# Adaptive layer norm, local attention and a mixture of experts: the set-up of the first batch and a program of its own for batch 0

## The reference

```python
mod = (_silu(L0_c) @ L0_wmod).reshape(L0_c.shape[0], 6, 1, -1)
sa, ca, ga, sb, cb, gb = (mod[:, 0], ..., mod[:, 5])
ga = (2 * (ga >= 0) - 1) * jnp.maximum(jnp.abs(ga), 0.25)
...
h = _layernorm(x, axis=-1) * (1 + ca) + sa
x_tran = jnp.matmul(h, W) + b
weights = jnp.einsum('bsd,btd->bst', x_tran, h)
lw = 1.0 / (location + EPS) * (location != 0)      # location = |i - j|
weights = jnp.exp(jnp.tanh(weights * lw))
weights = weights * off_diag
weights = weights / (jnp.sum(weights, axis=-1, keepdims=True) + EPS)
x = x + ga * jnp.matmul(weights, h)
h = _layernorm(x, axis=-1) * (1 + cb) + sb
x = x + gb * ffn(h)                                # top 2 of 8 experts, and a shared one
```

## Time and profile before

| | us |
|---|---|
| median of 3 runs | 718.41 |
| the three runs | 720.79, 718.41, 714.60 |
| the profiled execution | 714.96 |
| its span | 713.2 |
| PE busy | 633.7 (89%) |
| DVE busy | 472.6 (66%) |
| ACT busy | 400.2 (56%) |
| POOL busy | 371.6 (52%) |

### The profile page before, as it was taken

The page is one execution under the profiler, slowest core; times in us unless marked ns, Lnnn a source line. Parts: engine busy times, 40 slices in busy tenths (PEclk is TensorE's granted clock), DMA queues, the critical chain, the costliest instruction groups (busy, mean ns, idle before and its releaser), DMA issues.

```text
span 713.2 us, 13455 instructions
## 1 busy us (share of the span) xinstructions
PE 633.7 (89%) x4311; PEld 576.9 (81%) x4311; DVE 472.6 (66%) x1455; ACT 400.2 (56%) x639; POOL 371.6 (52%) x353
## 2 busy tenths in 40 slices
PE   2599898798888888887977999999999999999995
PEld 2398787688787777777966889998999899999995
DVE  6678997795959688686957357454454445444498
ACT  4568678474765757463531365556556555655441
POOL 4415254667566567577657126565655555556200
PEclk9889999898998999998987999999999999999998
DMA  8030000000010101010113726565666566530692
GB/s 302 0 150 1 1 2 23 15 31 31 24 37 20 35 12 39 23 39 31 35 45 113 259 84 205 175 201 166 202 188 199 185 184 203 168 105 31 233 372 118
DMA packets 29612, 76.44 MB, mean 107 GB/s; under 512 B 7110, under 2 KB 11358, under 8 KB 29440
## 3 DMA queue, kind: packets, MB, share of 16 engines
q1 hardware_dynamic: 20208, 58.49, 25.1%
q0 software_dynamic: 8640, 16.93, 6.7%
q10 hardware_dynamic: 720, 0.47, 0.2%
HBM read 53.53 MB, written 23.24 MB: 108 GB/s over the span
## 4 chain that ended last, share of the span: by engine, by line
PE 41%; DVE 33%; ACT 11%; issue 6%; another core or an unknown queue 6%; POOL 1%; DMA 1%; POOLq 0%; ACTq 0%; DVEq 0%; SPq 0%
PE value L1550 13%; PE score L1404 6%; PE score L1402 6%; PE score L1403 6%; PE misc L1550 6%; DVE work L957 5%; DVE stats L862 3%; ACT work L687 3%; ACT work L685 3%; PE value L1597 2%; PE value L1430 2%; DVE rows_all L980 2%; ACT w_ring L663 1%; DVE rows_all L945 1%
## 5 line engine op out<-in xcount | busy, mean ns | idle before, releaser
L632 POOL DMA_INDIRECT rows_z<-tile_y,tags x142 | 146.1, 1029 | 124.4 <-issue 42.9
L957 DVE TENSOR_TENSOR work<-score,lw 128x1024 f32<-128x1024 f32 x64 | 78.1, 1220 | 43.7 <-remote 30.1
L1430 PEld LDWEIGHTS value<-w_ring,work 128*128 128x128 f32 x768 | 98.3, 202 | 7.0 <-DVE work L963 3.5
L1402 PE MATMUL score<-h_hi,h_lo 128*128 128x512 f32 (+1 forms) x252 | 95.6, 380 | 8.2 <-issue 4.7
L1430 PE MATMUL value<-w_ring,work 128*128 128x129 f32 x768 | 99.3, 286 | 1.6 <-DVE work L963 1.6
L563 POOL DMA_INDIRECT rows_x<-work,slot x64 | 67.0, 1047 | 47.0 <-DVE work L957 15.5
L685 ACT ACTIVATE work<-work 128x1024 f32<-128x1024 f32 x64 | 67.3, 1052 | 43.0 <-DVE work L957 41.1
L1404 PE MATMUL score<-h_hi,h_lo 128*128 128x512 f32 (+1 forms) x252 | 90.1, 357 | 0.0
L1403 PE MATMUL score<-h_hi,h_lo 128*128 128x512 f32 (+1 forms) x252 | 89.8, 356 | 0.0
L769 ACT ACTIVATE work<-score,w_ring 128x512 f32<-128x512 f32 (+1 forms) x96 | 53.4, 617 | 61.5 <-PE score L1404 54.4
L769 ACT ACTIVATE work<-score,w_shared 128x512 f32<-128x512 f32 x64 | 40.3, 687 | 59.5 <-PE score L1404 29.7
(11 more groups left out here) (238 smaller groups left out, 1303.6 us busy)
## 6 DMA issues: line engine op xcount, KB each, us to landing
w_ring<-packs SPq DMA_DIRECT2D x24, 578.0 KB
rows_all<-packs SPq DMA_DIRECT2D x23, 578.0 KB
lw<-rows_x SPq DMA_DIRECT2D x24, 260.0 KB
res<-x SPq DMA_DIRECT2D x8, 512.0 KB, 5.6
h_t<-rows_z SPq DMA_DIRECT2D x4, 1024.0 KB, 8.0
mod<-mod_rows SPq DMA_DIRECT2D x1, 2560.0 KB, 10.2
rows_z<-tile_y,tags POOLq DMA_INDIRECT x142
rows_all<-rows_z SPq DMA_DIRECT2D x2, 1024.0 KB, 12.7
```

What stands on the lines that cost most here:

```text
L632: nc.gpsimd.indirect_dma_start(rows_z[:, :], bass.IndirectOffsetOnAxis(ap=tags[pos][:, k, 0:1].bitcast(I32), axis=0), tile_y[par][:, k, :] ...
L957: nc.vector.tensor_tensor(prob[:, t % 4, :].rearrange("p (h n) -> p h n", h=2), score[:, 2 * (t % 2):2 * (t % 2) + 2, :], lw[:, at:at + S] ...
L1402: nc.tensor.matmul(out, a_lo, b_hi, start=True, stop=False)
L1430: ins = nc.tensor.matmul(value[:, s // 3, c0:c0 + D + 1], prob[:, t % 4, s * P:(s + 1) * P], normal[b % 3][:, t, :], start=(t == 0 and s % ...
```

## The change

In the set-up, the 1024 columns of the reciprocals are cut into pieces of 128, 256, 256 and 384 columns (before 256, 384 and 384), and the last of them is moved behind the instructions that write `mod_col`. With the small one for the silu these are five reciprocals. The attention weight's high part (`watt_hi`) is written by ACT before the keys of batch 0, not after them. The moments of batch 1 and the shift formed from them go from ahead of the first `weigh` to behind the first and the second.

Batch 0 has a function of its own, `first_batch`, on ACT, DVE and PE, and the conditions on b == 0 in `batch` are gone. POOL's and SP's programs are the same.

```diff
@@ -699,19 +699,33 @@
                 act.wait_ge(gap_ready, b + 1)
                 nc.scalar.activation(gap_e[:, :], gap[:, :], ACT.Exp).then_inc(gap_exp, 1)
 
+            def first_batch(par):
+                weights(0, 0)
+                modulation()
+                weights(0, 1)
+                normalise(1)
+                weights(0, 2)
+                weights(0, 3)
+                transposed(1, 1 - par, 0)
+                weights(0, 4)
+                transposed(1, 1 - par, 1)
+                weights(0, 5)
+                queries(1, 1 - par, 0)
+                weights(0, 6)
+                queries(1, 1 - par, 1)
+                weights(0, 7)
+                normalise(2)
+
             def batch(b, par):
-                ahead_2 = [(0, 2), (2, 4), (4, 6), (6, 8)] if 0 < b < B - 2 else []
-                if exists(b + 1) and b > 0:
+                if b == 0:
...
-                if b == 0:
-                    normalise(b + 2)
 
             normalise(0, 0, G // 2)
             normalise(0, G // 2, G)
+            act.wait_ge(small_loaded, 48)
+            nc.scalar.activation(watt_hi[:, :], watt_sb[:, :], ACT.Copy).then_inc(watt_hi_ready, 1)
             act.wait_ge(col_ready, 1)
             for half in range(2):
                 transposed(0, 0, half, score[:, half, :])
-            act.wait_ge(small_loaded, 48)
-            nc.scalar.activation(watt_hi[:, :], watt_sb[:, :], ACT.Copy).then_inc(watt_hi_ready, 1)
             for half in range(2):
                 queries(0, 0, half, score[:, 2 + half, :])
             batches(act, batch)
@@ -889,7 +901,7 @@
             dve.wait_ge(distance_ready, 1)
             lw_chain(nc.vector.scalar_tensor_tensor(out=lw_from[:, :], in0=lw_from[:, :], scalar=-1.0, in1=lw_from[:, :], op0=ALU.mult, op1=ALU.max))
             lw_chain(nc.vector.tensor_scalar(lw_from[:, :], lw_from[:, :], EPS_ATT, None, ALU.add))
-            location_weights(0, 2 * P)
+            location_weights(0, P)
             moments_1(0)
 
             step = Chain(dve, silu_step, 0)
@@ -897,13 +909,14 @@
             step(nc.vector.tensor_scalar(silu[:, :], silu[:, :], 1.0, None, ALU.add))
             step(nc.vector.reciprocal(silu[:, :], silu[:, :]))
             nc.vector.tensor_tensor(silu[:, :], silu[:, :], c_sb[:, :], ALU.mult).then_inc(silu_ready, 1)
-            location_weights(2 * P, 5 * P)
+            location_weights(P, 3 * P)
             shift_1(0, 1)
-            location_weights(5 * P, S)
+            location_weights(3 * P, 5 * P)
 
             dve.wait_ge(col_ps_ready, 1)
             nc.vector.tensor_copy(mod_col[:, 0:2, :].rearrange("p m b -> p (m b)"), misc[:, 0:2 * B])
             nc.vector.tensor_scalar(mod_col[:, 2:4, :].rearrange("p m b -> p (m b)"), misc[:, 2 * B:4 * B], 1.0, None, ALU.add).then_inc(col_ready, 1)
+            location_weights(5 * P, S)
 
             def mirror(i):
 
@@ -932,10 +945,8 @@
             mirror(0)
             for half in range(2):
                 split_q(0, 0, half, score[:, 2 + half, :])
-            moments_1(1)
             dve.wait_ge(const_ready, 1)
             nc.vector.memset(den[:, :], 0.0)
-            shift_1(1, 2)
 
             def normalise_2(b, to=xhat2):
                 dve.wait_ge(ln2_rstd, b + 1)
@@ -1063,12 +1074,42 @@
                 dve.wait_ge(w_hi_ready, m + 1)
                 nc.vector.tensor_tensor(w1_lo[par], w[:, 0:F], w1_hi[par].bitcast(F32), ALU.subtract).then_inc(w_split, 1)
 
+            def first_batch(par):
+
+                weigh(0, 0)
+                moments_1(1)
+                weigh(0, 1)
+                shift_1(1, 2)
+                weigh(0, 2)
+                weigh(0, 3)
+                moments_1(2)
+                clear_diagonal(0, 0)
+                weigh(0, 4)
+                split_h(1, 1 - par, 0)
+                clear_diagonal(0, 1)
+                clear_diagonal(0, 2)
+                weigh(0, 5)
+                split_h(1, 1 - par, 1)
+                shift_1(2, 3)
+                clear_diagonal(0, 3)
+                weigh(0, 6)
+                split_q(1, 1 - par, 0)
+                moments_1(3)
+                clear_diagonal(0, 4)
+                weigh(0, 7)
+                split_q(1, 1 - par, 1)
+                moments_1(4)
+                clear_diagonal(0, 5)
+                clear_diagonal(0, 6)
+                clear_diagonal(0, 7)
+
+
             def batch(b, par):
+                if b == 0:
+                    return first_batch(par)
                 weigh(b, 0)
                 if exists(b - 2):
                     count_chosen(b - 2, route_chain[b - 2])
-                if b == 0:
-                    moments_1(2)
                 if b == 1:
                     moments_1(AHEAD)
                     shift_1(3, AHEAD)
@@ -1090,8 +1131,6 @@
                     moments_2(b - 1)
                 if exists(b + 1):
                     split_q(b + 1, 1 - par, 0)
-                if b == 0:
-                    moments_1(3)
                 if b == 1:
...
+                scores(0, par, 5)
+                values(0, par, 2)
+                queries(1, 1 - par, 0)
+                scores(0, par, 6)
+                values(0, par, 3)
+                queries(1, 1 - par, 1)
+                values(0, par, 4)
+                scores(0, par, 7)
+                values(0, par, 5)
+
             def batch(b, par):
-
-
+                if b == 0:
+                    return first_batch(par)
                 scores(b, par, 0)
                 if exists(b - 1):
                     values(b - 1, 1 - par, G - 2)
-                if b > 0 and exists(b + 1):
+                if exists(b + 1):
                     transpose_h(b + 1, 0)
                 scores(b, par, 1)
                 if exists(b - 1):
@@ -1465,13 +1521,8 @@
                         pe.wait_ge(ht_ready, 2 * b + 3)
                     ranks(b - 2)
                 scores(b, par, 2)
-                if b == 0:
-                    pe.wait_ge(mirrored, 2)
-                    transpose_h(1, 0)
                 if exists(b + 1):
                     transpose_h(b + 1, 1)
-                if b == 0:
-                    pe.wait_ge(mod_evac, 1)
                 scores(b, par, 3)
                 values(b, par, 0)
                 if exists(b + 1):
```

More of the change, by code:

```diff
@@ L700, in gap_exponent @@
                 nc.scalar.activation(gap_e[:, :], gap[:, :], ACT.Exp).then_inc(gap_exp, 1)
+            def first_batch(par):
[14 more added lines that the diff above has]
+                normalise(2)
             def batch(b, par):
-                ahead_2 = [(0, 2), (2, 4), (4, 6), (6, 8)] if 0 < b < B - 2 else []
-                if exists(b + 1) and b > 0:
+                if b == 0:
+                    return first_batch(par)
+                ahead_2 = [(0, 2), (2, 4), (4, 6), (6, 8)] if b < B - 2 else []
+                if exists(b + 1):
                     transposed(b + 1, 1 - par, 0)
                 weights(b, 0)
-                if b == 0:
-                    modulation()
-                    normalise(1)
                 if exists(b - 2):
@@ L712, in batch @@
                 weights(b, 1)
-                if b == 0:
-                    transposed(1, 1, 0)
                 if exists(b + 1):
@@ L1107, in batch @@
                     normalise_2(b - 1)
-                if b == 0:
-                    moments_1(4)
                 if b == 1:
                     moments_1(AHEAD + 2)
-                if b == 0:
-                    shift_1(2, 3)
                 weigh(b, 6)
@@ L1450, in ranks, with first_batch @@
                 nc.tensor.matmul(misc[:, 0:E], ones[:, :], carry[:, :], start=False, stop=True).then_inc(rank_ps_ready, 1)
+            def first_batch(par):
+                for t in range(4):
+                    scores(0, par, t)
+                pe.wait_ge(mod_evac, 1)
+                values(0, par, 0)
+                pe.wait_ge(mirrored, 2)
+                transpose_h(1, 0)
+                scores(0, par, 4)
+                values(0, par, 1)
+                transpose_h(1, 1)
+                scores(0, par, 5)
[7 more added lines that the diff above has]
+                values(0, par, 5)
             def batch(b, par):
+                if b == 0:
+                    return first_batch(par)
                 scores(b, par, 0)
```

2 lines of the change are left out of this document (removed).

## The result

The change takes 727.1 us in the median of four runs (723.93 to 732.16), the kernel before 719.6 (714.6 to 720.86): a ratio of 1.0119, interval 1.0061 to 1.0177. The profiled execution took 726.95 us (span 725.2), 12.0 more than that of before. The forecast was 724, within 716 to 731.

A forecast was written before the change was run, and what follows sets the result against it. PE, kept waiting by the chain of waits through DVE, POOL and ACT, was taken as the bound in batch 0; the terms sum to +6.9 us, 721.9 on the profiled 714.96, 725.3 on the median; forecast 724, range 716 to 731.

The forecast's parts named there:

- set-up, up to the first scores: Smaller reciprocal pieces and early watt_hi let PE's first scores start at 18.75 us: 2.5 us gained, 1.7 at the other end.
- detour behind the first weighing: Moments of batch 1 and POOL's root no longer precede the first weighing, now at 20.3 us against 25.56: 2.7 us gained.
- up to the second values: Batch 0: PE waits for diagonals behind DVE's moments and weighings, with low clock; lead falls to 3.8 us: 1.4 us lost.
- up to the fifth: Batch 0: fifth diagonal stands behind weighing, q_lo and moments of batch 3; lead becomes a lag of 1: 4.9 us lost.
- up to the sixth: Batch 0: sixth diagonal stands behind q_lo and moments of batch 4; values at 61.0 us against 55.38: 4.7 us lost.
- behind the shift additions: Start of batch 1: POOL's three additions hold DVE's shift until 71.2 us, delaying the second weighing: 1.3 us lost.
- The clock behind them: After PE waits of over 2 us in batch 0, the low clock: matmuls 0.43 us, not 0.23; values 3.1 us.
- rival in which the clock holds: PE's batch 0 waits may not all lower its clock: 6.3 us less, lag 0.6 or 3.8, median 721 us; chance 0.14.
- What stands at the mark goes through to the end: The lag at batch 2's second query product, 83.4 us against 76.87, reaches the end, as later work hangs on semaphores.
- the kept lead: Rival: diagonals find DVE free, so the first weighing's 5.2 us lead reaches the end: 713.2 us median; chance 0.05.
- stay low: Rival: PE's clock low from 25.5 us through third values and over 5 us after 61: 728 us median; chance 0.13.
- The lock of the root: Rival: POOL's 2.93 us root holds DVE's sixth diagonal, 3.2 us more: 728.5 us median; chance 0.03.

The follow-up runs named there:

- diagonals-first: The change with each DVE diagonal cleared once its exponential is there, moments of batches 2, 3, 4 behind diagonals 2, 5, 7: 683.5 us, ratio 0.9899 to the kernel before.
- first pair: Profiled executions of the kernel before and the change on the first chip: 714.96 and 726.95 us.
- second pair: The kernel before and the unaltered change profiled again on another chip: medians 690.12 and 697.41 us, ratio 1.0095.
- new set-up alone: The kernel before with only the change's reciprocal pieces and early watt_hi, batch 0 as before: 687.21 us, ratio 0.9949.
- moments of batch 2 late: The change with the moments of batch 2 moved from ahead of the first diagonal to behind the second: 692.69 us, ratio 1.0018 to the kernel before.
- moments of batch 4 late: The change with the moments of batch 4 moved from ahead of the sixth diagonal to behind the seventh: 695.8 us, ratio 1.006 to the kernel before.

## Why the prediction was right, step by step

The mechanism is the one predicted, and the diagonals-first run shows it rather than argues it. The sum was +6.9 and the mark stands at +5.7:

| step | predicted | measured, first pair |
|---|---|---|
| set-up, up to the first scores | -2.5 | -1.1 |
| detour behind the first weighing | -2.7 | -2.6 |
| up to the second values | +1.4 | +0.4 |
| up to the fifth | +4.9 | +3.3 |
| up to the sixth | +4.7 | +4.6 |
| up to batch 1's second scores | -0.2 | -0.1 |
| behind the shift additions | +1.3 | +1.1 |

The right column is the difference between the rows above and the marks of before (21.23, 25.56, 43.4, 52.2, 55.38, 62.13, 76.87), step by step.

- **Set-up.** Shift and normalisation came at 9.26 and 9.46 us, as walked (9.3, 9.4), and the first product at 15.05. But I carried the clock of before over to it: on the first chip its six matmuls took 0.43 us each and not 0.23, and the next product 2.06 us and not 1.46. The term was mis-sized by 1.4 us there; on the other chips it was larger than 2.5.
- **Detour.** Right as a step: the first weighing at 21.92 against 25.56. The time, 1.6 us behind the 20.3 predicted, is mostly the set-up's shortfall.
- **Waits.** 2.15, 3.87, 2.12, 1.37 and 4.38 us, against 2.5, 3.9, 2.3, 1.8 and 4.6.
- **The clock behind them.** This rule was wrong in part. I took one row, 2.63 us and then the low clock, and let each wait of over 2 us bring it. It fell behind 3.87 and 4.38 us and held behind 2.15 and 2.12: 1.2 us less in the fourth scores, 1.3 and 0.4 less behind the second values. The price I had for a slow stretch of values was a little low too: my 3.22 us row had the clock back before its end (the window from 176 to 177 us has 0.72), and the slow values here took 3.55 and 3.68. A part of the rival in which the clock holds was thus true, and it hid the shortfall of the set-up.
- **Sixth values.** 60.10 against 61.0, the lag turning exactly where the program has q_lo and the moments of batch 4 ahead of the diagonal.
- **Shift.** Held until 70.7 us (2.15 us; one of half the columns took 0.10), 71.2 predicted. POOL's timeline has the root and the three additions, which end at 70.68:

```profile
60.71 2.93 POOL L483 TENSOR_TENSOR rstd<-rstd,minus_half 128x16 f32<-128x16 f32 x1
63.61 7.07 POOL L540 TENSOR_TENSOR res<-res,mod 128x1024 f32<-128x1024 f32 x3
```

- **What stands at the mark goes through to the end.** True to 0.1 us for the diagonals-first kernel, and in the first pair to 2.2 us up to the last weighing, where it is 6.4. Then the first pair loses some 6 us more, which no step of mine had and most of which the second pair doesn't have. The mechanism gives 5.7 of the 7.5 us between the medians; the rest, and the 6 us of that pair, I can't assign.
- **Luck in the number.** The set-up gained 1.4 us less than its term, and between the first weighing and the fifth values 2.6 us less was lost than in the sum. These errors in part cancel, and the 1.8 us between the medians that no step has brought the time back to near the sum.

The rivals: the kept lead would have needed waits under 0.5 us at the fifth and sixth diagonals, and they were 1.37 and 4.38. It was a true picture of another order, though: with the diagonals first it came out 7.0 us faster than before. The clock did not stay low: the window from 42 to 56 us has 1.00. The lock of the root could not show at the sixth diagonal: the root began at 60.71, when the diagonals (59.78 and 0.66) were through. But the same trace has it in batch 1: POOL's root of 4.19 us runs from 93.39, and a diagonal at 93.82 and one at 96.71 take 0.28 us each, as the one at 53.05 did before. This root holds no diagonal.

## What to carry to other kernels

When an engine serves both the next batch and the engine that sets the end, list for each short operation that the latter wants (here 0.3 us) what is queued ahead of it on its own engine: 2.3 us of work for later, put in front of it, cost 2.4 and 5.3 us in the two places tried. An earlier start is only worth what the next hand-over passes on, so walk the marks up to where the order returns to the old one before you count the gain. A wait on PE costs its length and can cost a slow stretch behind it: avoiding two of them here, with the waits kept, gave back some 3 of 6.6 us.

## What the runs showed of the hardware

- The clock behind a wait is not fixed by the wait's length. Before the third scores it was low after 2.63 us and high after 2.62 us in the kernel with the new set-up alone (the matmul took 0.50 us and not 0.80); behind the first query product's wait it was high after 1.91 us and low after 1.90 in two executions of the kernel before. After 1.82 us, with the moments of batch 2 late, the values took 3.78 us; after 1.37 us 2.05 us, and after 1.38 us 3.17 on another chip. After 2.12 us they took 2.05, and after 2.17 us, with the moments of batch 4 late, 3.69. Behind the waits named here of 3.38, 3.87, 3.88, 4.38, 6.19, 7.26, 10.40 and 10.66 us it was low each time.
- Keeping PE multiplying through two of its waits, for nothing, kept the high level there and gained 3.2 us, though another stretch fell to the low one.
- The same kernel takes 719 us on one chip and 690 to 691 on others, with nearly equal waits in batch 0 (2.63 and 2.57, 1.64 and 1.62 us). The granted clock, averaged over the span, was 0.949 in the profiled execution against 0.964 to 0.973 there; what else differs was not looked into.
- A DVE diagonal and a shift are held by POOL's additions of 128 x 1024 (1.22 us for the diagonal at 56.72 before, 2.15 us for the shift at 68.56, until the additions end at 70.68) and not by POOL's root, which is as long or longer (0.28 us under a root of 4.19).
- One stall of 10.66 us on PE that ends with none of the profile's releasers ("issue") was seen in one execution of the change, beside 3.38 us at that place before. What it is stays open.
